# One chunk of a mixture's rows gathered behind a new wait, and normed before the next chunk is combined

## The chip, the cores and the metric

The kernel runs on one core of a Trainium2 chip. The metric is the device time of one execution in microseconds (us). The core has five engines with instruction streams of their own: TensorE (PE, with its weight loads as PEld), VectorE (DVE), ScalarE (ACT), GpSimd (POOL) and SyncE (SP, which here issues most of the DMA transfers). They wait for each other through semaphores that the kernel writes out by hand.

## The reference

Six layers are applied to an input x of 8 x 64 tokens of width 256. Each reads a layer norm of x and adds its result to x. The two that matter here are the third, a mixture of experts, and the fourth, an attention to the context with a mask:

```python
# x: (8, 64, 256) = 512 tokens; ctx_1024: (8, 1024, 256)
diff = x[:, :, None, :] - keys                      # 16 experts
logits = -jnp.sum(diff * diff, -1) + x @ rw.T + rb
topv, topi = jax.lax.top_k(logits, 4)
w = jax.nn.softmax(topv, axis=-1)
hidden = gelu(einsum('bld,efd->blef', x, w1) + b1)  # F = 1024
exp_out = einsum('blef,edf->bled', hidden, w2) + b2
fused = sum(w[..., None] * take_along_axis(exp_out, topi), axis=2)
...
logits = where(mask == 0, NEG, q @ k.T / 16)        # k = v = ctx_1024, q = layernorm(x)
out = layernorm(softmax(logits) @ v) * gamma + beta
```

## The kernel before

The 512 tokens are four chunks of 128 (TC = 4, numbered t or p). X holds x, 128 partitions by four chunks.

**The mixture.** Tokens are sorted to their experts in tiles of 128 rows. There are 31 tiles (TILES), and each has 8 units (UNITS) of a first product (`up`), a gelu on ACT (line 1298, semaphore gelu_done, one count a unit) and a second product (`down`). The first 29 tiles (COLD = 29) are copied to an SBUF tile and stored to y_slots in HBM by POOL (`store_tile`, semaphores y_stored, one for each of four buffers). The last two tiles never go to HBM: ACT takes them to SBUF (`take_last`, semaphore last_taken) and PE adds them to the chunks by a product with a spread of the gates (`add_last`). That sum lies in two banks. When the second `add_last` is done, bias_done has its counts, and DVE adds the banks to X (`add_sums`, line 2008: first chunk 0 alone, then chunks 1 to 3).

What was stored comes back by **gathers**: `gather_rows(t)` issues four indirect DMAs on POOL (one for each of a token's four experts, 128 rows of 1 KB each, line 995) that read y_slots into y_rows, and count gathered[t]. `combine(t)` on DVE waits for gathered[t] and adds the four to chunk t of X with their gates, one after the other (line 1980).

**The next attention.** For each chunk: `norm_begin(4, t)` on DVE takes the statistics (lines 1546, 1550, 1554), POOL raises the variance to the power -1/2 (`rstd_of(4, t)`, line 699), and `arrive(t)` on DVE makes the normed chunk xn (line 1558) and adds beta to X (line 2015). PE turns xn (line 2551), ACT takes it to xnT (line 1247), and PE makes the scores of chunk p from xnT and ctxT2[p] (`score2`, 16 products of 512 columns); `greatest(p)` on DVE finds their maximum (line 1986), ACT takes the exponent (line 1317), PE turns the weights (line 2738), ACT takes them to SBUF (line 1324), PE multiplies by ctxN2[p] (`mix2`, 32 products), and `normalise(p)` and `leave(p)` on DVE norm the result and begin the next layer. The order on ACT is by hand too: the exponent of chunk 2 (`weights2(2)`) stands ahead of `take_tokens(3)`, so xnT of chunk 3 waits for the maximum of chunk 2. On PE the order is: scores 0, scores 1, weights 0 turned, mix 0, weights 1 turned, scores 2, mix 1, scores 3, weights 2 turned, mix 2. The scores of chunk 0 are preceded by a few products that only keep PE running (`keep_running`).

**The context.** SP loads each chunk's part as two transfers of 2 MB: `context_T(p)` (line 600, for the scores) and `context_N(p)` (line 604, for the mix). T(0) and N(0) go behind tiles 26 and 27. T(1) goes when the last row tile has been stored. T(2) and N(1) go when gathered[2] has its count. T(3), N(2) and N(3) go when all four chunks of X are combined (x_updated, raised by DVE after `combine(3)`).

Of the kernel before, what the change touches and what calls it, by code (L numbers as in the profile page):

```python
# [32 lines left out]
E0, TOP0, F0 = 16, 4, 1024  # L33
# [7 lines left out]
UNITS = FC  # L41
OVER = E0 - 1
TILES = E0 + OVER
WB, HB, YB = 5, 4, 4
# [79 lines left out]
def part(tile, layout, name):  # L124
    a, b = layout[name]
    return tile[:, a:b]
# [29 lines left out]
def build(nc, d, out):  # L156
    ctx = ExitStack()
    with ctx:
        names = set()

        def sem(name):
            assert name not in names
            names.add(name)
            return ctx.enter_context(nc.semaphore(name))
# [300 lines left out]
        y_stored = [sem(f"y_stored{k}") for k in range(YB)]  # L465
        gathered = [sem(f"gathered{t}") for t in range(TC)]
# [8 lines left out]
        up_done, gelu_done, down_done = sem("up_done"), sem("gelu_done"), sem("down_done")  # L475
# [70 lines left out]
        def y_stores(k):  # L546

            return 16 * len(range(k, COLD, YB))

        def norm_of(k, t):  # L550

            return TC * (k - 1) + t + 1
# [23 lines left out]
        def _(sp):  # L576
# [12 lines left out]
            def expert(i):  # L589
                if i < E0:  # L590
                    of = d["w0"][i]
                else:
                    if i == E0:
                        sp.wait_ge(slots_ready, 2)
                    e = sp.value_load(owner[0:1, i - E0:i - E0 + 1], min_val=0, max_val=E0 - 1)
                    of = d["w0"][bass.ds(e, 1)].rearrange("a p n -> p (a n)")
                sp.dma_start(raw[i % WB][:], of).then_inc(raw_loaded[i % WB], 16)

            def context_T(p):
                sp.dma_start(ctxT2[p][:], d["ctxT"][2 * p:2 * p + 2].rearrange("b p c n -> p b c n"))\  # L600
                    .then_inc(ctxT2_loaded[p], 16)

            def context_N(p):
                sp.dma_start(ctxN2[p][:], d["ctxN"][2 * p:2 * p + 2].rearrange("b p k n -> p b k n"))\
                    .then_inc(ctxN2_loaded[p], 16)
# [15 lines left out]
            def masks(of):  # L621
                for m in of:
                    sp.dma_start(mask[m][:], d["mask"][m * P:(m + 1) * P]).then_inc(mask_loaded, 16)
# [7 lines left out]
            def slot_rows(k):  # L631
                a, b = X_PIECES[k:k + 2]
                sp.dma_start(x_rows[:, a - ROWS_FROM:b - ROWS_FROM, :], x_slots.rearrange("(t p) n -> p t n", p=P)[:, a:b, :]).then_inc(rows_loaded[k], 16)
# [3 lines left out]
            for i in range(TILES):  # L637
                sp.wait_ge(down_done, UNITS * (i + 1))
                if i and i + WB < TILES:
                    expert(i + WB)  # L640
                if i == PLAIN:
                    sp.wait_ge(spread_turned, share_before + LAST)
                    slot_rows(2)
                if i == TILES - WB:
                    masks(range(2, TC))
                if i == TILES - WB:
                    context_T(0)
                if i == TILES - WB + 1:
                    context_N(0)
                if i == COLD - 1:  # L650
                    sp.wait_ge(y_stored[i % YB], 16 * (i // YB + 1))
                    context_T(1)

            sp.wait_ge(gathered[2], 16 * TOP0)
# [38 lines left out]
        def _(pool):  # L693
            order = Order(pool, pool_step)

            def rstd_of(k, t):

                pool.wait_ge(var_ready, norm_of(k, t))
                nc.gpsimd.tensor_tensor(rstd[:, t:t + 1], vareps[:, t:t + 1], part(table, TABLE, "minus_half")[:, 0:1], ALU.pow)\
                    .then_inc(rstd_ready, 1)  # L700
# [291 lines left out]
            def gather_rows(t, places=range(TOP0)):  # L992
                for j in places:
                    k = TOP0 * t + j
                    nc.gpsimd.indirect_dma_start(y_rows[:, k, :], None, y_slots, bass.IndirectOffsetOnAxis(slots[:, k:k + 1], 0))\
                        .then_inc(gathered[t], 16)
# [10 lines left out]
            for k in range(YB):  # L1007
                pool.wait_ge(y_stored[k], y_stores(k))
            gather_rows(0)
            gather_rows(1)  # L1010
            pool.wait_ge(last_taken, last_before + LAST)
            gather_rows(2, range(2))
            rstd_of(4, 0)
            gather_rows(2, range(2, 3))
            rstd_of(4, 1)
            gather_rows(2, range(3, TOP0))
            gather_rows(3)
            rstd_of(4, 2)
            rstd_of(4, 3)
# [96 lines left out]
        def _(act):  # L1116
# [75 lines left out]
            def last_batch(b):  # L1192
                second_half(b - 1, 6)
                weights1(b, 0)
                second_half(b - 1, 7)
                weights1(b, 1)
                _, c, half = KEY_TURN[0]
                key_piece(key_at(b, 0), c, half)
                for d in range(1, DUOS):
                    both_halves(b, 2 * d - 2)  # L1200
                    weights1(b, 2 * d)
                    weights1(b, 2 * d + 1)
                    second_half(b, 2 * d - 1)
                    if d == 1:
                        take_front(0)
                        take_front(1)
                for half in range(2):
                    turned_half1(b, 6, half, LAST_TURN_BANKS[half], sixth_ready)
                second_half(b, 7)
# [332 lines left out]
        def _(dve):  # L1542
            order = Order(dve, dve_step)

            def norm_stats(k, t):
                nc.vector.bn_stats(stats[:, t, :], X[:, t, :]).then_inc(stats_ready, 1)

            def norm_moments(k, t):
                dve.wait_ge(stats_ready, norm_of(k, t))
                nc.vector.bn_aggr(moments[:, t, :], stats[:, t, :]).then_inc(moments_ready, 1)  # L1550

            def norm_variance(k, t):
                dve.wait_ge(moments_ready, norm_of(k, t))
                nc.vector.tensor_scalar_add(vareps[:, t:t + 1], moments[:, t, 1:2], EPS).then_inc(var_ready, 1)

            def norm_tile(k, t):
                dve.wait_ge(rstd_ready, norm_of(k, t))
                nc.vector.tensor_scalar(xn[:, t, :], X[:, t, :], moments[:, t, 0:1], rstd[:, t:t + 1],  # L1558
                                        ALU.subtract, ALU.mult).then_inc(xn_ready, 1)
# [8 lines left out]
            def norm_begin(k, t):  # L1568

                norm_stats(k, t)  # L1570
                norm_moments(k, t)
                norm_variance(k, t)
# [127 lines left out]
            def last_batch(b, par):  # L1700
# [6 lines left out]
                norm_tile(2, 2)  # L1707
                gather(b - 1, 1 - par, 0)
                _, c, half = KEY_TURN[0]
                key_piece(4 * b + len(FIRST_BANKS) + 1, c, half)  # L1710

# [265 lines left out]
            def combine(t):  # L1977
                dve.wait_ge(gathered[t], 16 * TOP0)
                for j in range(TOP0):
                    order.step(nc.vector.scalar_tensor_tensor(X[:, t, :], y_rows[:, TOP0 * t + j, :], gate_top[:, t, j:j + 1],  # L1980
                                                              X[:, t, :], ALU.mult, ALU.add))
# [24 lines left out]
            def add_sums(a, b):  # L2006
                dve.wait_ge(bias_done, (b + 1) // 2)
                order.step(nc.vector.tensor_tensor(X[:, a:b, :], X[:, a:b, :],
                                                   banks[:, 2:4, :].rearrange("p a (t n) -> p (a t) n", n=D)[:, a:b, :], ALU.add))

            def arrive(t):

                norm_tile(4, t)
                dve.wait_ge(xn_ready, norm_of(4, t))
                order.mark(nc.vector.tensor_tensor(X[:, t, :], X[:, t, :], part(rows, ROWS, "beta"), ALU.add))
# [4 lines left out]
                norm_tile(5, p)  # L2020

            combine(0)
            combine(1)
            add_sums(0, 1)
            norm_begin(4, 0)
            add_sums(1, TC)
            norm_begin(4, 1)
            arrive(0)
            arrive(1)
            greatest(0)  # L2030
            combine(2)
# [236 lines left out]
        def _(pe):  # L2268
# [157 lines left out]
            def last_batch(b, par):  # L2426
# [3 lines left out]
                weigh(b - 1, 1 - par, 0, 2)  # L2430
                turn(b - 1, 7)
                _, c, half = KEY_TURN[0]
                project_keys(key_at(b, 0), b, par, c, half)
                weigh(b - 1, 1 - par, 0, 3)
# [700 lines left out]
```

## Time and profile before

| | |
|---|---|
| median of 3 runs | 719.49 us (719.39 to 720.48) |
| the profiled execution | 718.73 us |
| its span in the trace | 716.9 us |
| PE busy | 678.7 us, 95% of the span |
| DVE, POOL, ACT busy | 544.9, 451.1, 413.8 us |
| HBM read, written | 111.77 MB, 10.81 MB |
| TensorE clock granted, mean | 0.992 |

The span is the stretch between the first and the last instruction of the trace; the 1.8 us beside it lie around it. The busy times are sums over the whole execution. The change sits in one stretch of some 60 us (480 to 540 us from the span's start), so the rows further down are from there. "T(2)" below is the transfer that `context_T(2)` issues, and so on; "gather 2.0" is the first of the four of `gather_rows(2)`.

### The profile page before, as it was taken

What the parts mean: (1) busy time and instruction counts of PE and PEld (TensorE: products, weight loads), DVE (VectorE), ACT (ScalarE), POOL (GpSimd) and SP (SyncE); (2) the same over time, 40 slices, a digit from 0 to 9 for tenths busy, and PEclk for the clock granted to TensorE, in tenths of its full rate; (3) what the DMA queues carried; (4) which work ended last, traced back from release to release, by engine and by line L of the source; (5) the groups of instructions that cost most, each with busy time, mean ns of one, the idle gap of its engine ahead of it and who ended that gap; (6) DMA issues with size and microseconds to landing.
All of it is one profiled execution on the core that took longest, in us unless ns stands there. A gap on an engine that the chain in (4) does not pass through costs nothing.

```text
span 716.9 us, 15536 instructions
## 1 busy us (share of the span) xinstructions
PE 678.7 (95%) x5712; PEld 555.4 (77%) x5712; DVE 544.9 (76%) x1212; ACT 413.8 (58%) x790; POOL 451.1 (63%) x487
## 2 busy tenths in 40 slices
PE   6899999999999978899999999999999899999998
PEld 3677777777877767799999999997457466666687
DVE  5878778787889675477777777763658899999577
ACT  3665756656755652376766766652335886665441
POOL 4848634547486734768999777835414699898130
PEclk9999999999999999999999999999999999999999
DMA  8301101001007464499999999995784620001000
GB/s 339 129 2 60 60 1 59 22 37 59 0 0 299 180 278 193 169 372 406 427 382 350 332 336 346 337 356 187 288 348 155 214 83 0 1 1 45 1 0 30
DMA packets 20365, 123.38 MB, mean 172 GB/s; under 512 B 2304, under 2 KB 6672, under 8 KB 13008
## 3 DMA queue, kind: packets, MB, share of 16 engines
q1 hardware_dynamic: 17376, 114.59, 41.6%
q0 software_dynamic: 2928, 8.00, 3.0%
q8 instruction: 35, 0.57, 0.3%
q14 instruction: 26, 0.21, 0.1%
HBM read 111.77 MB, written 10.81 MB: 171 GB/s over the span
## 4 chain that ended last, share of the span: by engine, by line
PE 78%; DVE 11%; ACT 5%; issue 3%; POOL 1%; another core or an unknown queue 1%; DMA 1%; DVEq 0%; SPq 0%; ACTq 0%; PEldq 0%; POOLq 0%
PE banks L2270 67%; PE banks L2338 8%; DVE shown L2136 2%; PE banks L2902 2%; ACT probs L1147 1%; DVE negmax_raw L1666 1%; DVE spread L1911 1%; PE banks L2579 1%; ACT banks L1437 1%; DVE banks L2143 1%; DMA table<-in_table 1%; DVE xn L1558 1%; PE banks L2738 0%; POOL q_heads_hi L711 0%
## 5 line engine op out<-in xcount | busy, mean ns | idle before, releaser
L2270 PE MATMUL banks<-xT,raw 128*128 128x128 f32 x992 | 151.4, 276 | 5.5 <-DVE xT L1921 4.9
L2270 PEld LDWEIGHTS banks<-xT,raw 128*128 128x128 f32 x992 | 134.5, 192 | 8.7 <-issue 6.8
L972 POOL TENSOR_TENSOR w_lo<-raw,w_hi 128x1024 fp32r<-128x1024 f32 x52 | 122.7, 2385 | 7.6 <-ACT w_hi L1267 7.2
L1298 ACT ACTIVATE banks<-banks,later 128x128 f32<-128x128 f32 x208 | 70.5, 340 | 56.6 <-PE banks L2270 55.4
L1930 DVE CAST mid_hi<-banks 128x128 fp32r<-128x128 f32 x208 | 60.1, 289 | 37.1 <-ACT banks L1298 34.9
L1177 ACT ACTIVATE probsT<-banks 128x512 f32<-128x512 f32 x68 | 40.1, 598 | 74.8 <-PE banks L2338 74.5
L1047 POOL TENSOR_TENSOR inject<-BCbc,drive 128x1024 f32<-128x1024 f32 x31 | 72.8, 2361 | 11.3 <-DVE shown L2136 6.3
L1147 ACT ACTIVATE probs<-banks,negmax 128x1024 f32<-128x1024 f32 x64 | 71.2, 1113 | 11.9 <-DVE negmax L1668 10.0
L1666 DVE TENSOR_REDUCE negmax_raw<-banks 128x1 f32<-128x1024 f32 x64 | 77.5, 1212 | 0.5 <-PE banks L2270 0.3
L2270 PE MATMUL banks<-w_hi,mid_hi 128*128 128x256 f32 x208 | 75.5, 363 | 0.0
L2338 PE MATMUL banks<-table,probs 128*128 128x128 f32 x512 | 69.6, 279 | 0.4 <-DVE probsT L1639 0.4
L2338 PEld LDWEIGHTS banks<-table,probs 128*128 128x128 f32 x512 | 55.1, 141 | 16.9 <-issue 14.0
L1932 DVE TENSOR_TENSOR mid_lo<-banks,mid_hi 128x128 fp32r<-128x128 f32 x208 | 60.6, 292 | 7.1
L2270 PE MATMUL banks<-w_hi,mid_lo 128*128 128x256 f32 x208 | 58.6, 282 | 0.0
L2270 PE MATMUL banks<-w_lo,mid_hi 128*128 128x256 f32 x208 | 58.5, 281 | 0.0
L1267 ACT ACTIVATE w_hi<-raw 128x1024 fp32r<-128x1024 f32 x52 | 54.6, 1050 | 0.0
L732 POOL TENSOR_TENSOR ctx_lo<-ctx_raw,ctx_hi 128x1024 fp32r<-128x1024 f32 x14 | 34.2, 2450 | 23.0 <-ACT ctx_hi L1133 22.9
L1437 ACT ACTIVATE banks<-delta,exp_a 128x512 f32<-128x512 f32 x64 | 41.6, 683 | 8.1 <-DVE shown L2153 6.0
L1639 DVE COPY probsT<-banks 128x512 f32<-128x512 f32 x60 | 41.2, 687 | 1.5 <-PE banks L2338 1.5
L1620 DVE SCALAR_TENSOR_TENSOR k_lo<-banks,bk,k_hi 128x512 fp32r<-128x512 f32 x32 | 23.8, 747 | 21.5 <-ACT k_hi L1139 21.5
L2270 PE MATMUL banks<-probsT,V 128*32 128x128 f32 x1024 | 40.0, 277 | 0.0
L2270 PEld LDWEIGHTS banks<-w_hi,mid_hi 128*128 128x128 f32 x208 | 39.9, 192 | 0.0
(362 smaller groups left out, 1709.6 us busy)
## 6 DMA issues: line engine op xcount, KB each, us to landing
raw<-in_w SPq DMA_DIRECT2D x31, 2048.0 KB, 9.3
ctx_raw<-in_ctxT SPq DMA_DIRECT2D x8, 1024.0 KB, 4.8
ctxT<-in_ctxT SPq DMA_DIRECT2D x4, 2048.0 KB, 9.0
ctxN<-in_ctxN SPq DMA_DIRECT2D x4, 2048.0 KB, 13.8
x_slots<-zero SPq DMA_DIRECT2D x1, 3968.0 KB, 12.6
y_slots<-y_tile POOLq DMA_DIRECT2D x29, 128.0 KB, 7.0
wf<-in_w SPq DMA_DIRECT2D x9, 384.0 KB, 5.9
BCbc<-bc_rows SPq DMA_DIRECT2D x6, 512.0 KB, 7.1
```

The source lines that it names most:

```text
L972: nc.gpsimd.tensor_tensor(w2_lo[i % WB][:, cols], raw[i % WB][:, EW // 2:][:, cols], w2_hi[i % 2][:, cols].bitcast(F32), ALU.subtract).the ...
L1047: nc.gpsimd.tensor_tensor(inject[g % 2][:], Bbc[:, GS * g:GS * (g + 1), :], over(drive[:, m, :], GS, 1), ALU.mult).then_inc(inject_ready, 1)
L1147: nc.scalar.activation(probs[i % 2][:], two(i % 2), ACT.Exp, bias=negmax[i % 2][:], scale=0.25, accum_out=sums[i // PAIRS][:, i % PAIRS:i ...
L1267: nc.scalar.activation(w2_hi[i % 2][:, cols], raw[i % WB][:, EW // 2:][:, cols], ACT.Copy).then_inc(w2_hi_ready, 1)
L1298: nc.scalar.activation(to, held, ACT.Gelu, bias=b1[:, bass.ds(at + u, 1)]).then_inc(gelu_done, 1)
L1437: last = nc.scalar.activation(two(HELD_BANKS[g % 2])[:, s * TOK:(s + 1) * TOK], delta[:, m, :], ACT.Copy, scale=exp_a[:, at:at + 1])
L1639: nc.vector.tensor_copy(probsT[c][:, 0:KC // 2, j, :], pb(5).rearrange("p (k n) -> p k n", n=P))\
L1666: nc.vector.tensor_reduce(negmax_raw[i % 2][:], two(i % 2), AX.X, ALU.max, negate=True).then_inc(raw_max, 1)
L1930: nc.vector.tensor_copy(mid_hi[n % HB][:], held).then_inc(mid_hi_ready, 1)
L1932: nc.vector.tensor_tensor(mid_lo[n % HB][:], held, mid_hi[n % HB][:].bitcast(F32), ALU.subtract).then_inc(mid_lo_ready, 1)
L2270: return nc.tensor.matmul(o, lhsT, rhs, start=start, stop=stop)
L2338: last = nc.tensor.transpose(pb(banks[half])[:, k * P:(k + 1) * P], probs[i % 2][:, kc * P:(kc + 1) * P], ident)
```

## The change

SP waits for the landing of chunk 0's gathers, not for the last store of a tile, before it issues T(1). POOL waits between the gathers of chunk 0 and those of chunk 1 until all but three gelus of the mixture are done. POOL's `rstd_of(4, 0)` moves from behind gather 2.1 to ahead of gather 2.0, and `rstd_of(4, 1)` from behind gather 2.2 to behind gather 2.1. DVE combines chunk 1 only after chunk 0 is normed and `arrive(0)` is done. No work is added or taken away.

```diff
@@ SP
                 if i == COLD - 1:
-                    sp.wait_ge(y_stored[i % YB], 16 * (i // YB + 1))
+                    sp.wait_ge(gathered[0], 16 * TOP0)
                     context_T(1)
@@ POOL
             gather_rows(0)
+            pool.wait_ge(gelu_done, TILES * UNITS - 3)
             gather_rows(1)
+            rstd_of(4, 0)
             pool.wait_ge(last_taken, last_before + LAST)
             gather_rows(2, range(2))
-            rstd_of(4, 0)
-            gather_rows(2, range(2, 3))
             rstd_of(4, 1)
-            gather_rows(2, range(3, TOP0))
+            gather_rows(2, range(2, TOP0))
             gather_rows(3)
@@ DVE
             combine(0)
-            combine(1)
             add_sums(0, 1)
             norm_begin(4, 0)
             add_sums(1, TC)
+            arrive(0)
+            combine(1)
             norm_begin(4, 1)
-            arrive(0)
             arrive(1)
             greatest(0)
             combine(2)
```

POOL's instructions from the last two stores on, before (-) and after (+), where the lines L995 are the gathers:

```order
 L990 DMA y_slots<-y_tile_141 128x256
 L990 DMA y_slots<-y_tile_138 128x256
-L995 DMA y_rows<-y_slots,slots 128x256 x10
-L699 TENSOR_TENSOR rstd<-vareps,table 128x1
-L995 DMA y_rows<-y_slots,slots 128x256
-L699 TENSOR_TENSOR rstd<-vareps,table 128x1
-L995 DMA y_rows<-y_slots,slots 128x256 x5
+L995 DMA y_rows<-y_slots,slots 128x256 x8
+L699 TENSOR_TENSOR rstd<-vareps,table 128x1
+L995 DMA y_rows<-y_slots,slots 128x256 x2
+L699 TENSOR_TENSOR rstd<-vareps,table 128x1
+L995 DMA y_rows<-y_slots,slots 128x256 x6
```

Ten gathers stood ahead of the first rstd and eight do now; six gathers, not five, stand behind the second.

DVE's instructions from chunk 0's statistics on; the three rows of line 1546, 1550 and 1554 that move are chunk 1's:

```order
 L1554 TENSOR_SCALAR vareps<-moments 128x1
 L2008 TENSOR_TENSOR X<-X,banks 128x768
-L1546 BN_STATS stats<-X 128x6
-L1550 BN_AGGR moments<-stats 128x2
-L1554 TENSOR_SCALAR vareps<-moments 128x1
 L1558 TENSOR_SCALAR xn<-X,moments,rstd 128x256
 L2015 TENSOR_TENSOR X<-X,rows 128x256
+L1980 SCALAR_TENSOR_TENSOR X<-y_rows,gate_top,X 128x256 x4
+L1546 BN_STATS stats<-X 128x6
+L1550 BN_AGGR moments<-stats 128x2
+L1554 TENSOR_SCALAR vareps<-moments 128x1
 L1558 TENSOR_SCALAR xn<-X,moments,rstd 128x256
```

Chunk 1's four additions and its statistics now stand between chunk 0's `arrive` and its own; the four stood ahead of `add_sums` before.

## Rows read from the trace of the kernel before

**Rows 1.** The page's first part: busy time of the engines.

```profile
PE 678.7 (95%) x5712; PEld 555.4 (77%) x5712; DVE 544.9 (76%) x1212; ACT 413.8 (58%) x790; POOL 451.1 (63%) x487
```

**Rows 2.** The chain that ended last: start us, us, what.

```profile
494.12 0.72 issue
...
528.36 3.65 PE banks L2270 x16
```

**Rows 3.** Timeline of PE and PEld: start us, us, engine, line, [idle before <-releaser].

```profile
503.24 0.38 PEld L2551 LDWEIGHTS banks<-table,xn 128*128 128x128 f32 x2 [0.43 <-DVE xn L1558]
...
508.01 0.44 PE L2551 MATMUL banks<-table,xn 128*128 128x128 f32 x2
...
523.77 3.65 PE L2270 MATMUL banks<-ctxN,probsT 128*64 128x256 f32 x32
```

**Rows 4.** Timeline of POOL.

```profile
484.42 1.05 POOL L995 DMA_INDIRECT y_rows<-y_slots,slots  x1 [3.18 <-DMA y_slots<-y_tile]
...
488.29 0.95 POOL L995 DMA_INDIRECT y_rows<-y_slots,slots  x1 [0.30 <-issue]
...
498.82 0.96 POOL L995 DMA_INDIRECT y_rows<-y_slots,slots  x1 [4.58 <-ACT y_tile L1280]
...
501.22 0.57 POOL L699 TENSOR_TENSOR rstd<-vareps,table 128x1 f32<-128x1 f32 x1 [0.18 <-DVE vareps L1554]
501.97 0.99 POOL L995 DMA_INDIRECT y_rows<-y_slots,slots  x1 [0.18 <-issue]
...
503.80 0.99 POOL L995 DMA_INDIRECT y_rows<-y_slots,slots  x1 [0.18 <-issue]
...
508.88 0.95 POOL L995 DMA_INDIRECT y_rows<-y_slots,slots  x1 [0.30 <-issue]
```

**Rows 5.** Timeline of DVE.

```profile
494.83 4.13 DVE L1980 SCALAR_TENSOR_TENSOR X<-y_rows,gate_top,X 128x256 f32<-128x256 f32 x8 [10.83 <-DMA y_rows<-y_slots,slots]
499.85 0.42 DVE L2008 TENSOR_TENSOR X<-X,banks 128x256 f32<-128x256 f32 x1 [0.88 <-PE banks L2270]
...
501.06 0.94 DVE L2008 TENSOR_TENSOR X<-X,banks 128x768 f32<-128x768 f32 x1
...
502.78 0.40 DVE L1558 TENSOR_SCALAR xn<-X,moments,rstd 128x256 f32<-128x256 f32 x1
...
515.70 2.05 DVE L1980 SCALAR_TENSOR_TENSOR X<-y_rows,gate_top,X 128x256 f32<-128x256 f32 x4 [0.80 <-DMA y_rows<-y_slots,slots]
...
518.57 0.15 DVE L1554 TENSOR_SCALAR vareps<-moments 128x1 f32<-128x1 f32 x1
...
524.34 1.22 DVE L1986 TENSOR_REDUCE stat<-banks 128x1 f32<-128x1024 f32 x1
```

**Rows 6.** Timeline of ACT.

```profile
494.43 0.37 ACT L1298 ACTIVATE mid<-banks,later 128x128 f32<-128x128 f32 x1 [2.87 <-PE banks L2270]
...
525.78 1.11 ACT L1317 ACTIVATE probs<-banks,stat 128x1024 f32<-128x1024 f32 x1 [5.61 <-DVE stat L1987]
...
527.83 0.38 ACT L1247 ACTIVATE xnT<-banks 128x256 f32<-128x256 f32 x1 [0.84 <-PE banks L2551]
```

**Rows 7.** Timeline of SP's DMA issues: T(1), then N(1).

```profile
484.21 0.37 SPq L600 DMA_DIRECT2D ctxT<-in_ctxT  x1
...
507.07 0.51 SPq L604 DMA_DIRECT2D ctxN<-in_ctxN  x1
```

**Rows 8.** DMA issues, 500 to 512 us: size, us to landing.

```profile
ctxT<-in_ctxT SPq DMA_DIRECT2D x1, 2048.0 KB, 9.0
ctxN<-in_ctxN SPq DMA_DIRECT2D x1, 2048.0 KB, 14.5
```

**Rows 9.** Stretches: busy PE, PEld, DVE, ACT, POOL; PE clock, DMA share, GB/s.

```profile
283.00:284.70 1.70, 0.00 (x0) 0.00 (x0) 0.54 (x3) 0.37 (x1) 0.00 (x0) 1.00 0.21 77
292.10:295.10 3.00, 0.00 (x0) 0.00 (x0) 2.91 (x4) 0.00 (x0) 2.84 (x2) 1.00 0.69 295
296.50:299.50 3.00, 3.00 (x12) 2.64 (x11) 0.00 (x0) 0.74 (x2) 2.08 (x4) 0.50 0.27 96
```

## The prediction

> **What bounds the kernel now.** I read the page's busy times first: PE is busy 95% of the span [rows 1], so time is lost or won only where PE waits. Then the chain of waits through the stretch that the change touches, 480 to 540 us. It stays on PE but for short steps over ACT. Two pieces matter. At 494.12 PE stands for 0.72 us, and at 528.36 the scores of chunk 3 begin [rows 2]. Then the timelines, engine by engine, for how much room each supplier of PE has.
>
> Six facts come out of them. (a) In the last tile ACT is idle for 2.87 us ahead of a gelu at 494.43 [rows 6]. The row names PE as releaser, but PE's product for it was done long before. The 0.72 us of PE just ahead are its echo. Those are the microseconds in which T(1), issued at 484.21 [rows 7], and eight gathers, issued from 484.42 on [rows 4], share the DMA engines. (b) DVE's first additions start at 494.83, when gather 0.3, issued at 488.29 to 489.24, has landed [rows 4, 5]. They end at 498.96 and then wait 0.88 us for PE's bank, so their late start costs nothing. (c) Chunk 0's xn is ready at 503.18 and its weight load at 503.24 waited for it [rows 3, 5]. (d) POOL issues gather 2.0 at 498.82, gather 2.3 at 503.80 and gather 3.3 at 508.88 [rows 4]. (e) T(2) and N(1) leave when gather 2.3 has landed, N(1) at 507.07. It lands 14.5 us later, at 521.6 [rows 7, 8], and PE wants it at 523.77 [rows 3]: 2.2 us of room. (f) Gather 3.3 was issued by 509.83, yet `combine(3)` had to wait for its landing until 515.70 [rows 4, 5]. From there DVE runs on, with only its trips to POOL between, to `greatest(2)` at 524.34 [rows 5]. ACT's exponent follows at 525.78 to 526.89, and ACT takes chunk 3's tokens at 527.83 [rows 6]: 0.9 us of room.
>
> **The change part by part.** I time it as if PE stood where it stands before, and subtract a gain at the end.
>
> *T(1) behind gathered[0].* Gathers that meet no transfer land about 1.8 us after their issue ends: gather 2.3 ends at 504.79 and the issues of T(2) and N(1), which wait for it, follow 0.4 us apart, N(1) at 507.07 [rows 4, 7]. So gathers 0.0 to 0.3 land near 491.1 and T(1) goes then, not at 484.21. With the 9.0 us of T(2) [rows 8] it lands near 500, against its first use behind 508.01 [rows 3]. The cover is 8 us. Free.
>
> *The gelu wait.* The counted gelu is the one ahead of the stall, done near 491.6. Gather 1.0 goes at 491.6, not 489.54 (four spacings of 1.25 on from 484.42), and 1.3 is issued by 496.4. It meets T(1). The worst the trace shows for that is the 5.9 us of gather 3.3, which met T(2) and N(1); at that price chunk 1's rows are there at 502.3, and with no meeting at 498.2. Needed: 502.9 (below). Free, with 0.6 us of cover at the bad end.
>
> *What the two may give.* If the stall of (a) comes of the crowded DMA engines, it shrinks: at 491 to 493 only the head of T(1) is under way. The gain is between 0 and the 0.72 us of PE. No row says which, and I take 0.4.
>
> *Chunk 0 normed first.* `arrive(0)` no longer has chunk 1's statistics ahead of it. `add_sums` ends at 502.0 [rows 5], so xn is ready at 502.4, not 503.18. PE's weight load had waited 0.43 us [rows 3]. This gives PE up to 0.4 us at 503, but everything PE wins here it loses again if it must wait later for something that does not move with it. It is not in the sum.
>
> *POOL's queue.* This is the term that counts. `rstd_of(4, 0)` waits for DVE, which waits for PE's bank; it ran at 501.22 and cannot run sooner [rows 4, 5]. Gather 2.0 was ahead of it at 498.82 and is behind it now. It goes 0.75 us after it, at 501.97, and 2.1 at 503.2. Then `rstd_of(4, 1)` waits for chunk 1: DVE ends `add_sums` at 502.0, xn 0.40 and beta about as much to 502.9, four additions of 2.05 in all to 504.9, statistics 0.95 (517.75 to 518.72) [rows 5] to 505.9. The rstd runs then, and gather 2.2 goes at 506.6, 2.3 at 507.9 and 3.3 five-quarter microseconds times four later, at 512.9. Before they were 503.80 and 508.88: **both are 4.0 us later**. Six gathers are queued behind the wait, and T(2), N(1) and the end of X behind them. (Chunk 1's own xn comes at 507.0, still ahead of 508.01.)
>
> *What is late next.* T(2) and N(1) leave 4.0 us later. T(2) lands near 519.7, just ahead of its use at 520.3. N(1) lands at 525.6, against 523.77: PE waits 1.8 us, and mix 1 ends that much later. Gather 3.3 stands to T(2) as before (3.0 goes 1.6 us ahead of it, 3.1 0.3), so it meets the same crowd and lands 4.0 us later, at 519.7. `combine(3)` and all of (f) move by 4.0, the exponent of chunk 2 ends at 530.9, ACT takes chunk 3's tokens then, not at 527.83, and the scores of chunk 3 start at 531.5, not 528.36. That is 4.0 - 0.9 = **3.1 us later**, and it contains the 1.8 of N(1): behind mix 1 PE waits the other 1.3. T(3) goes at 521.8 and by the 9.0 lands at 530.8, just in time. Behind that PE's own chain follows one for one.
>
> *Sum.* 3.1 - 0.4 = +2.7 us. Bank, rstd and gathers all start from PE's last `add_last`, so a gain of 0.4 there moves them all. The profiled execution of before took 718.73 us (span 716.9), which gives 721.4; the median of the runs is 0.76 above it, so I forecast **722.2**. Bounds of the unknowns: a gain of 0 gives 722.6, of 0.72 gives 721.9; chunk 1's rows landing later than 502.9 would add their excess.
>
> **A rule against a row.** Gather 3.3 took 5.9 us from the end of its issue to its use, with 4 MB of context issued from 3.2 us before its issue ended [rows 4, 5, 7]. This is a row and the sum goes by it. If small transfers took turns fairly with large ones they would land in about the 1.8 us of (e), at 511.6 before and 515.7 after; then (f) would not move at all. The Trainium skill, DMA: Bandwidth & Descriptors, section "Queues, rings and completion order", says that each DMA engine goes round its queues a packet at a time. By that rule gather 3.3 would not be late and the sum would be N(1)'s 1.8 us alone. The trace does not agree as to the landing, 5.9 us against 1.8.
>
> **The rivals.**
> *Only N(1) is late.* The gathers of chunk 3 could slip in ahead of T(2) by a race of tenths of a microsecond, and land by 515.7. Then +1.8 less the 0.4: 720.9. Against: the spacing of the issues is the same within 0.1 us.
> *The clock falls.* PE was idle from 292.10 to 295.10, and in 296.50 to 299.50 its clock was 0.50, half of full speed, 1.2 GHz; after 1.7 idle microseconds at 283 it stayed at 2.4 GHz [rows 9]. Three microseconds at half clock cost 1.5: 723.8. Here the gaps are 1.8 and 1.3 with work between, nearer the one that kept the clock. The Trainium skill, TensorE: Matmul & The Clock Gate, section "Part 1: The HAM clock gate", has idleness as what closes the gate; which of the two gaps ours resembles only rows can tell.
> *Not slower.* The stall at 494 vanishes (-0.72), the earlier xn gives its 0.4, and the 4 us of POOL are hidden. For that N(1) would have to land in 12.7 us instead of 14.5 and gather 3.3 in 2.7 instead of 5.9, that is, the DMA engines would have to be emptier than before. It decides if POOL's delay stays under 0.9 us, the room of (f). Time: 718.4, or a little below if the gelus gain more.
> *No change at all in the order that matters:* excluded, POOL's stream shows the gathers behind the rstd.
>
> **How the numbers follow.** A run of this kernel can tell about 0.2%, 1.4 us, from no change: 718.1 to 720.9. Both waits, 721.9 to 722.7: 0.56. Only N(1): 0.14, on the border, half in "same". Clock: 0.10. Not slower: 0.20, of which 0.08 beyond 0.2%. So faster 0.08, same 0.19, slower 0.73. The range leaves out most of the last case and the far end of the clock's: 720.2 to 724.2.
>
> **What would show it.** Right: gathers 2.0 and 3.3 at about 501.6 and 512.5; DVE's `combine(3)` starting near 519.3; PE idle some 1.8 us ahead of mix 1 for the context and 1.3 ahead of the scores of chunk 3 for ACT; PE's 0.72 us at 494 smaller; the clock at 1.00. Wrong: `combine(3)` at 516, N(1) landing by 523, or the chain of waits still without a gap between 504 and 532.

## The result, and the profile after

The changed kernel takes **720.89 us**, the median of 20 runs (719.37 to 723.11), beside 718.70 us for the kernel before, the median of 20 runs on the same chip (717.36 to 721.13): ratio 1.003, 95% interval 1.002 to 1.004. It is slower by 2.2 us; the forecast was +2.7 in the profiled execution and 722.2 us for the median.

718.70 is 0.8 below the median shown ahead of the prediction, so differences say more here than absolute times. The profiled execution of the changed kernel is the slowest of its 20, 723.11 us with a span of 721.3. Part of that has nothing to do with the change: T(0) is issued at 470.01 us, against 467.58 before, though the program is the same up to there. Positions are therefore compared from an event, not from the start: from T(0)'s issue, or, where the prediction counts that way, from DVE's first addition of PE's bank (499.85 before [rows 5], 501.29 after).

PE of the changed kernel: start us, us, engine, line, [idle before <-releaser].

```profile
498.55 1.03 PE L2270 MATMUL banks<-raw,mid 128*128 128x256 f32 x4
500.05 1.99 PE L2270 MATMUL banks<-y_tile,spreadT 128*128 128x256 f32 x8 [0.47 <-ACT y_tile L1280]
...
505.87 3.65 PE L2270 MATMUL banks<-ctxT,xnT 128*64 128x512 f32 x16 [0.56 <-ACT xnT L1247]
...
510.46 3.65 PE L2270 MATMUL banks<-ctxT,xnT 128*64 128x512 f32 x16
...
517.40 3.67 PE L2270 MATMUL banks<-ctxN,probsT 128*64 128x256 f32 x32 [2.26 <-ACT probsT L1324]
...
523.20 3.65 PE L2270 MATMUL banks<-ctxT,xnT 128*64 128x512 f32 x16 [0.42 <-ACT xnT L1247]
527.00 3.67 PE L2270 MATMUL banks<-ctxN,probsT 128*64 128x256 f32 x32
```

The four groups of ctxT are scores 0 (505.87), 1 (510.46), 2 (523.20) and, below in the chain, 3; the two of ctxN are mix 0 (517.40) and mix 1 (527.00). The 0.72 us of PE [rows 2] are gone. There is a new wait of 2.26 us ahead of mix 0, where the kernel before waits 0.83 for the same probsT. Mix 1 shows no wait worth a row, although its context landed at the last moment (below).

POOL, then DVE, then ACT of the changed kernel:

```profile
494.26 0.94 POOL L995 DMA_INDIRECT y_rows<-y_slots,slots  x1 [1.94 <-ACT mid L1298]
495.51 1.07 POOL L995 DMA_INDIRECT y_rows<-y_slots,slots  x1 [0.30 <-issue]
...
502.66 0.57 POOL L699 TENSOR_TENSOR rstd<-vareps,table 128x1 f32<-128x1 f32 x1 [3.59 <-DVE vareps L1554]
503.42 0.99 POOL L995 DMA_INDIRECT y_rows<-y_slots,slots  x1 [0.18 <-issue]
504.71 0.96 POOL L995 DMA_INDIRECT y_rows<-y_slots,slots  x1 [0.31 <-issue]
507.26 0.57 POOL L699 TENSOR_TENSOR rstd<-vareps,table 128x1 f32<-128x1 f32 x1 [1.59 <-DVE vareps L1554]
508.02 0.99 POOL L995 DMA_INDIRECT y_rows<-y_slots,slots  x1 [0.18 <-issue]
...
514.35 0.95 POOL L995 DMA_INDIRECT y_rows<-y_slots,slots  x1 [0.30 <-issue]
```

```profile
501.29 0.42 DVE L2008 TENSOR_TENSOR X<-X,banks 128x256 f32<-128x256 f32 x1 [5.02 <-PE banks L2270]
...
521.00 2.05 DVE L1980 SCALAR_TENSOR_TENSOR X<-y_rows,gate_top,X 128x256 f32<-128x256 f32 x4 [3.90 <-DMA y_rows<-y_slots,slots]
```

```profile
494.50 0.37 ACT L1298 ACTIVATE mid<-banks,later 128x128 f32<-128x128 f32 x1 [0.51 <-PE banks L2270]
...
496.26 0.37 ACT L1298 ACTIVATE mid<-banks,later 128x128 f32<-128x128 f32 x1 [0.51 <-PE banks L2270]
...
515.22 0.60 ACT L1324 ACTIVATE probsT<-banks 128x512 f32<-128x512 f32 x1 [2.39 <-PE banks L2738]
516.65 0.60 ACT L1324 ACTIVATE probsT<-banks 128x512 f32<-128x512 f32 x1 [0.84 <-PE banks L2738]
```

Gather 3.3 is issued at 514.35, 13.06 us behind the bank's first addition; before it was 508.88, 9.03 behind [rows 4, 5]. `combine(3)` starts 19.71 behind it, not 15.85. The page's DMA view for the stretch 505 to 520 us of the changed kernel gives N(1), issued at 512.56, 14.4 us to its landing, that is 526.96, and mix 1's weight load waited for it:

```profile
ctxN<-in_ctxN SPq DMA_DIRECT2D x1, 2048.0 KB, 14.4
```

```profile
527.00 3.22 PEld L2270 LDWEIGHTS banks<-ctxN,probsT 128*64 128x64 f32 x32 [1.02 <-DMA ctxN<-in_ctxN]
```

The chain that ended last (start us, us, what) tells the same in one piece. Where before it kept to PE but for short steps over ACT, it now leaves PE at the bank's addition and comes back only at scores 3:

```profile
500.05 1.15 PE banks L2270 x4
501.29 0.43 DVE X L2008
...
507.26 0.57 POOL rstd L699
507.83 0.18 issue
508.02 0.99 POOL y_rows L995
...
514.35 6.63 DMA y_rows<-y_slots,slots
521.00 0.50 DVE X L1980
...
532.30 0.28 ACT xnT L1247
532.58 0.14 issue
532.72 3.65 PE banks L2270 x16
```

The account, in us from T(0)'s issue. The last column is gather 3.3's own issue. "Last additions" is PE's second `add_last`.

| kernel (T(0) issued at) | last additions | scores 0 | mix 0 | scores 2 | mix 1 | scores 3 | gather 3.3 |
|---|---|---|---|---|---|---|---|
| before (467.58) | 31.03 | 36.84 | 46.94 | 52.74 | 56.19 | 60.78 | 41.30 |
| after (470.01) | 30.04 | 35.86 | 47.39 | 53.19 | 56.99 | 62.71 | 44.34 |

One microsecond (0.99) is won by the last additions. Behind them 2.92 are lost in three places: 1.43 at mix 0 (scores 1 are still 0.98 ahead), 0.35 at mix 1 and 1.13 at scores 3. The net, 62.71 - 60.78 = 1.93, stands beside the 2.19 of the medians.

### The profile page after: what moved, and what is told of

The parts are those of the page before. It is cut to its first block, busy times and chain, and to the rows that moved or that the text cites. A ratio compares the mean times of both kernels' runs of the same rounds, so it can differ in the third digit from the quotient of the medians.

```text
span 721.3 us, 15536 instructions
## 1 busy us (share of the span) xinstructions
PE 680.7 (94%) x5712; PEld 556.6 (77%) x5712; DVE 540.9 (75%) x1212; ACT 413.7 (57%) x790; POOL 450.5 (62%) x487
## 4 chain that ended last, share of the span: by engine, by line
PE 76%; DVE 12%; ACT 4%; issue 3%; DMA 2%; POOL 1%; another core or an unknown queue 1%; DVEq 0%; SPq 0%; ACTq 0%; PEldq 0%
PE banks L2270 64%; PE banks L2338 8%; DVE shown L2136 2%; PE banks L2902 2%; DMA ctx_raw<-in_ctxT 1%; ACT probs L1147 1%; DVE negmax_raw L1666 1%; DMA y_rows<-y_slots,slots 1%; PE banks L2579 1%; DVE xn L1558 1%; ACT banks L1437 1%; POOL y_rows L995 1%; DVE banks L2143 1%; POOL rstd L699 1%
## 5 line engine op out<-in xcount | busy, mean ns | idle before, releaser
L2270 PEld LDWEIGHTS banks<-w_lo,mid_hi 128*128 128x128 f32 x208 | 40.2, 193 | 0.0
```

The costliest lines, as they stand in the source:

```text
L2270: return nc.tensor.matmul(o, lhsT, rhs, start=start, stop=stop)
```

## The experiments

Ratios are to the kernel before, run beside it on the same chip, with the 95% interval. "Changed" in a heading means that the edit is made to the changed kernel, otherwise to the kernel before. Their medians of the kernel before were 718.56 (22 runs), 719.24 (23) and 719.80 (29) us.

**order_only: changed, without the two waits.** T(1) goes behind `y_stored` as before, and POOL does not wait for a gelu.

```diff
-                    sp.wait_ge(gathered[0], 16 * TOP0)
+                    sp.wait_ge(y_stored[i % YB], 16 * (i // YB + 1))
-            pool.wait_ge(gelu_done, TILES * UNITS - 3)
```

> The change without its two waits on transfers: T(1) goes behind the last store and gathers 0 and 1 run through, as before; the order of DVE and POOL is the changed one. Theory A (the loss is POOL's queue: gathers 2.2 to 3.3 stand behind the rstd of chunk 1; the gain is that T(1) no longer crowds the last tile): gather 3.3 about 4.0 us later than in the kernel before, counted from the bank that DVE waits for, combine(3) as much, and no gain at the last tile, so +2.9 us, ratio 1.004. Rival B (the loss comes from chunk 1's gathers and T(1) meeting between 495 and 503): no loss, ratio 1.000 within 0.1%.

Measured 721.8 us (7 runs), ratio 1.0038 [1.0023, 1.0053]. The whole loss is there without the waits: it sits in the order of POOL and DVE. The last additions come 0.47 earlier than before, not 0.99 (none was expected), and ACT's stall at the last gelus is there (2.04, 1.10 and 1.10 us). In its profiled execution the clock rival shows itself: PE stands 2.06 us ahead of mix 0 and then does the 32 products in 5.36 us, not 3.67. Beside them the columns of the stretch (busy PE, PEld, DVE, ACT, POOL; PE clock, DMA share, GB/s), for this kernel and then for the profiled execution of the changed one over the same products, which it did at full clock:

```profile
517.47 5.36 PE L2269 MATMUL banks<-ctxN,probsT 128*64 128x256 f32 x32 [2.06 <-ACT probsT L1323]
```

```profile
517.50:520.80 3.30, 3.30 (x20) 2.41 (x22) 0.00 (x0) 0.92 (x2) 0.00 (x0) 0.61 1.02 416
```

```profile
517.50:520.80 3.30, 3.30 (x32) 2.51 (x31) 0.00 (x0) 0.85 (x2) 0.00 (x0) 1.00 1.03 418
```

**filled: changed, with the gathers spread around the two rstds.** DVE's order and both waits stay. Three gathers still stand behind chunk 1's rstd, but POOL does not stand idle ahead of it: no other could have gone first without making the rstd late.

```diff
             gather_rows(0)
             pool.wait_ge(gelu_done, TILES * UNITS - 3)
             gather_rows(1)
-            rstd_of(4, 0)
             pool.wait_ge(last_taken, last_before + LAST)
             gather_rows(2, range(2))
-            rstd_of(4, 1)
+            rstd_of(4, 0)
             gather_rows(2, range(2, TOP0))
-            gather_rows(3)
+            gather_rows(3, range(1))
+            rstd_of(4, 1)
+            gather_rows(3, range(1, TOP0))
```

> The changed kernel with one thing altered: POOL's two rstds are put where they fall due, rstd of chunk 0 behind gather 2.1 and that of chunk 1 behind gather 3.0, so that the gathers of chunks 2 and 3 run in the time in which POOL waited. Theory A: gather 2.3 and 3.3 come as early, from the bank, as in the kernel before (3.3 within 0.5 us), PE's idle time ahead of the scores of chunk 3 is gone, and the gain at the last tile is left: 0.7 to 1.0 us faster than before, ratio 0.999. Rival B: +2.2 us as in the changed kernel. Rival C (the rstd of chunk 1, about 1 us later than due, holds up the scores of chunk 1): +0.5.

Measured 717.77 us (11 runs), ratio 0.9988 [0.9975, 1.0001]. Gather 3.3 is issued 40.56 us behind T(0), 3.8 earlier than in the changed kernel, and all of PE's positions in the table lie 0.97 or 0.98 before those of the kernel before: last additions 30.05, scores 0 35.86, mix 0 45.96, scores 2 51.76, mix 1 55.22, scores 3 59.80. Mix 0 and scores 3 of filled:

```profile
514.56 3.67 PE L2271 MATMUL banks<-ctxN,probsT 128*64 128x256 f32 x32 [0.83 <-ACT probsT L1325]
...
528.40 3.65 PE L2271 MATMUL banks<-ctxT,xnT 128*64 128x512 f32 x16
```

So with the gathers early the 2.92 us are not lost at all, and the 0.99 stay won to the end. The wait for the gelu, T(1) late and chunk 0 first cost nothing.

**dose: changed, with all gathers of chunk 2 behind chunk 1's rstd.** Two more gathers are held.

```diff
-            gather_rows(2, range(2))
             rstd_of(4, 1)
-            gather_rows(2, range(2, TOP0))
+            gather_rows(2)
```

> The changed kernel with a larger dose: rstd of chunk 1 stands ahead of all gathers of chunk 2, so gathers 2.0 and 2.1 wait too. Theory A: gathers 2.3 and 3.3 another 2.5 us later, and the end with them one for one: +4.5 to +4.9 us against before, ratio 1.0065. Rival B: as the changed kernel, 1.003.

Measured 724.95 us (5 runs), ratio 1.0087 [1.0069, 1.0105]: +6.4 us. Gather 3.3 is issued at 46.92 behind T(0), 2.6 later than changed, and scores 3 come at 66.18, 3.5 later. More than the dose asks, and the trace shows the rest: T(2) is now late too, and scores 2 run at half clock behind the gap.

```profile
520.74 5.35 PE L2269 MATMUL banks<-ctxT,xnT 128*64 128x512 f32 x16 [2.35 <-DMA ctxT<-in_ctxT]
...
532.64 3.65 PE L2269 MATMUL banks<-ctxT,xnT 128*64 128x512 f32 x16 [2.26 <-ACT xnT L1246]
```

So the forecast of 4.5 to 4.9 us was too small. Scores 3, behind a gap of 2.26 us, ran at full clock.

**sp_only: T(1) behind gathered[0], nothing else.** The test of what the prediction called the cause of the stall.

```diff
-                    sp.wait_ge(y_stored[i % YB], 16 * (i // YB + 1))
+                    sp.wait_ge(gathered[0], 16 * TOP0)
```

> The kernel before with only T(1) moved behind gathered[0]. Theory A: ACT's idle time of 2.9 us in the last tile falls to the 0.5 us of its neighbours and PE's 0.7 us with it, nothing else moves: 0.5 to 1.0 us faster, ratio 0.999. Rival D (ACT's idle time has another cause and its absence in the changed kernel was chance): 1.000. Against both: if gather 1 meets T(1) and lands after DVE needs chunk 1, up to +1.

Measured 722.44 us (10 runs), ratio 1.0054 [1.0034, 1.0075]. A miss. T(1) leaves at 492.46, in the middle of ACT's stall, and the stall is not smaller but larger. ACT and then PE of sp_only:

```profile
495.84 0.37 ACT L1298 ACTIVATE mid<-banks,later 128x128 f32<-128x128 f32 x1 [3.83 <-PE banks L2270]
```

```profile
496.26 0.70 PE L2270 MATMUL banks<-raw,mid 128*128 128x256 f32 x2 [1.68 <-ACT mid L1298]
...
507.96 5.35 PE L2270 MATMUL banks<-ctxT,xnT 128*64 128x512 f32 x16 [0.57 <-ACT xnT L1247]
```

It loses once more behind: the rows of chunk 1 now meet T(1), DVE takes them in the old order ahead of chunk 0's sums, and scores 0 come late, behind a gap of 1.91 us ahead of chunk 0's xn, and at half clock. The move of T(1) alone is harmful; it needs chunk 0 normed first.

**gelu_only: POOL's wait for the gelu, nothing else.**

```diff
             gather_rows(0)
+            pool.wait_ge(gelu_done, TILES * UNITS - 3)
             gather_rows(1)
```

> The kernel before with only the gelu wait between the gathers of chunk 0 and chunk 1; T(1) goes early, as before, and meets the gathers of chunk 0. Theory E (ACT's idle time in the last tile comes with the gathers of chunk 1 being issued then, not with T(1)): ACT's 2.9 us and PE's 0.7 us are gone although T(1) is early. Rival F (it comes with T(1)): they stay. Either way chunk 1's rows land near 498.5, its four additions stand ahead of the bank's, and chunk 0's xn comes about 0.5 to 1.5 us late: 1.000 to 1.002 by theory E, 0.001 more by rival F.

Measured 720.01 us (12 runs), ratio 1.0013 [1.0002, 1.0024]. T(1) leaves early, at 485.72, and the stall is gone all the same. ACT there, with no idle time over 0.51 us from 491 to 495 (the 2.63 us ahead of the gelu at 490.15 stand in every kernel, before and after, at that gelu):

```profile
491.90 0.37 ACT L1299 ACTIVATE mid<-banks,later 128x128 f32<-128x128 f32 x1 [0.24 <-PE banks L2271]
492.78 0.37 ACT L1299 ACTIVATE mid<-banks,later 128x128 f32<-128x128 f32 x1 [0.51 <-PE banks L2271]
```

The last additions come 0.62 earlier, and the kernel is no faster, because chunk 1's rows, later now, hold up chunk 0 in the old order: its xn comes 1.06 us late for PE at 504.79.

**calm: both waits in the old order.** The diff is that of sp_only and gelu_only together.

> Both waits of the change, with the order of DVE and POOL as before. Chunk 1's rows meet T(1) and land 2.0 us behind the bank that DVE waits for, as in the trace of the changed kernel, and here chunk 0 cannot be normed before they are added. Theory G (the reorder on DVE is what lets the two waits be had): chunk 0's xn 4 us later, PE idle for about 3 us behind its running products, ratio 1.004 to 1.007, worse than the changed kernel. Rival: PE's running products cover most of it, 1.001.

Measured 723.74 us (6 runs), ratio 1.0058 [1.0038, 1.0078]. No stall, last additions 1.0 earlier, and then PE waits for chunk 0's xn long enough to come back at half clock:

```profile
506.79 0.69 PE L2552 MATMUL banks<-table,xn 128*128 128x128 f32 x2 [3.71 <-DVE xn L1559]
508.04 6.08 PE L2271 MATMUL banks<-ctxT,xnT 128*64 128x512 f32 x16 [0.56 <-ACT xnT L1248]
```

filled has the same two waits with chunk 0 first (and chunk 1's rstd two gathers later on POOL), and stands at 0.9988, some 5 us below the 1.0058 of calm. So chunk 0 first, which the sum counted as nothing, is worth about that much once both waits are in; no run moves it alone.

**filled_nowait: filled, without the wait for the gelu.**

```diff
-            pool.wait_ge(gelu_done, TILES * UNITS - 3)
```

> The kernel with the filled queue of POOL (rstds placed where due), T(1) behind gathered[0], DVE's changed order, but without the gelu wait. Theory E: ACT's idle time of 2 to 4 us in the last tile is back and PE loses 0.7 to 1.7 us there: 1.000 to 1.001 against before, 0.001 to 0.002 worse than the filled one. Rival F (it comes with T(1), which is late here): as the filled one, 0.999.

Measured 719.72 us (12 runs), ratio 1.0012 [0.9998, 1.0027]. ACT stands again at the last gelus, 2.10 and 2.48 us, and the last additions come at 31.34, 1.29 later than in filled.

```profile
492.18 0.37 ACT L1298 ACTIVATE mid<-banks,later 128x128 f32<-128x128 f32 x1 [2.10 <-issue]
495.03 0.37 ACT L1298 ACTIVATE mid<-banks,later 128x128 f32<-128x128 f32 x1 [2.48 <-remote]
```

**filled_m6: filled, with the wait three gelus earlier.** POOL hardly waits (gather 1.0 starts 0.30 us behind 0.3).

```diff
-            pool.wait_ge(gelu_done, TILES * UNITS - 3)
+            pool.wait_ge(gelu_done, TILES * UNITS - 6)
```

> The filled kernel with the gelu wait at all but six gelus instead of all but three, so that chunk 1's gathers start about 1 us or more earlier and two or three of them are issued ahead of the three gelus at which ACT stood idle. Theory E2 (ACT stands when gathers have been issued just ahead of that point): part of ACT's idle time is back and PE loses 0.2 to 0.7 us: 0.999 to 1.000. Rival (only a full queue of eight gathers does it): as the filled one, 0.9988.

Measured 720.37 us (12 runs), ratio 1.0012 [0.9997, 1.0028], 2.2 us above filled, which ran beside it (filled_again below). The stalls are back (1.49, 2.52 and 1.09 us), last additions at 31.41. So it is not enough that a wait is there: it must make POOL pause. As POOL's eight gathers went out without a pause here, as in filled_nowait, the run does not tell whether fewer than eight would do it, which it was meant to. The traces give 1.36 us of the 2.2; the rest has no row.

**late_ctx: changed, with T(2) and N(1) behind gathered[3].** It separates the two things that the prediction hung on POOL: the issue of gather 3.3, and what it meets.

```diff
-            sp.wait_ge(gathered[2], 16 * TOP0)
+            sp.wait_ge(gathered[3], 16 * TOP0)
```

> The changed kernel with T(2) and N(1) held until gather 3.3 has landed. Theory H (gather 3.3 lands late because the context's 4 MB are issued ahead of the last three gathers): it lands about 1.8 us after its issue ends instead of 5.7, and combine(3) starts 4 us earlier; T(2) and N(1) leave about 4 us later and PE waits for them, 1.5 to 3 us: 1.004 to 1.006. Rival (queues take turns, the landing is late for another reason): combine(3) starts as in the changed kernel and the waits come on top, 1.008.

Measured 723.86 us (6 runs), ratio 1.0064 [1.0047, 1.0082]. POOL, DVE and PE of late_ctx:

```profile
512.77 0.95 POOL L995 DMA_INDIRECT y_rows<-y_slots,slots  x1 [0.30 <-issue]
```

```profile
515.56 2.05 DVE L1980 SCALAR_TENSOR_TENSOR X<-y_rows,gate_top,X 128x256 f32<-128x256 f32 x4
```

```profile
515.71 5.36 PE L2270 MATMUL banks<-ctxN,probsT 128*64 128x256 f32 x32 [2.15 <-ACT probsT L1324]
...
524.43 3.65 PE L2270 MATMUL banks<-ctxT,xnT 128*64 128x512 f32 x16 [1.66 <-DMA ctxT<-in_ctxT]
529.40 3.67 PE L2270 MATMUL banks<-ctxN,probsT 128*64 128x256 f32 x32 [1.31 <-DMA ctxN<-in_ctxN]
```

Alone on the DMA engines, gather 3.3 is used 1.8 us after its issue ended (513.72 to 515.56), where in the changed kernel it took 5.7 (515.30 to 521.00). The price is that the context comes late in three places (the third, ahead of scores 3, is 0.47 us), and mix 0 runs at half clock.

This kernel is the changed one up to the last gelus, with both waits, and yet ACT stands at them. Its gathers of chunk 0 went out about 1 us later, so POOL paused for 0.98 us, not 1.94. The last additions come at 30.61, not 30.04. POOL, then ACT:

```profile
492.11 0.95 POOL L995 DMA_INDIRECT y_rows<-y_slots,slots  x1 [0.98 <-issue]
```

```profile
492.90 0.37 ACT L1298 ACTIVATE mid<-banks,later 128x128 f32<-128x128 f32 x1 [1.06 <-PE banks L2270]
494.41 0.37 ACT L1298 ACTIVATE mid<-banks,later 128x128 f32<-128x128 f32 x1 [1.14 <-PE banks L2270]
```

**filled_again and changed_again: the same two kernels once more, side by side.**

> The filled kernel once more, beside the changed kernel on one chip. Theory A: 0.9988 again, within 0.001, so that both together exclude 1. Rival: its first result was chance, 1.000.

> The changed kernel itself, beside the filled one. 1.003 as measured before; by theory A it is 2.9 to 3.1 us above the filled one.

Measured 718.14 us (12 runs), ratio 0.9973 [0.9957, 0.9989], and 720.57 us (12 runs), ratio 1.0015 [0.9999, 1.0031]. filled beats both kernels, the changed one by 2.4 us where 2.9 to 3.1 were expected. The changed kernel itself came out only 0.8 us above the kernel before, with an interval that just includes 1, where the first 20 runs gave 2.2 us; the two intervals overlap. The second profiled execution of the changed kernel differs from the first at one place: mix 0 ran at half clock.

```profile
514.53 5.36 PE L2270 MATMUL banks<-ctxN,probsT 128*64 128x256 f32 x32 [2.21 <-ACT probsT L1324]
...
530.30 3.65 PE L2270 MATMUL banks<-ctxT,xnT 128*64 128x512 f32 x16 [0.34 <-ACT xnT L1247]
```

Its scores 3 come at 63.06 from T(0), against 62.71: the 1.7 us of half clock fill most of what PE would have waited for ACT there.

## Why the prediction was right, and where it was not

*POOL's queue: right, and to a tenth.* Forecast from the bank's addition: gather 2.3 at 8.05 us and 3.3 at 13.05; measured 8.03 and 13.06. The six gathers stand behind chunk 1's rstd, 4.03 us late. filled issues three of them ahead of it, so that gather 3.3 goes 0.74 earlier than before, and the loss is gone; dose adds two and it grows. This is the cause, shown both ways.

*Gather 3.3 meets the same crowd: right.* `combine(3)` was forecast 4.0 later and is 3.86 later; late_ctx shows that it is the 4 MB of context that make 5.7 us out of 1.8. The rule against the row, turns of a packet at a time in the Trainium skill, DMA: Bandwidth & Descriptors, section "Queues, rings and completion order", had gather 3.3 land in time; the row decided rightly here.

*What is late next: right in place and size.* From the bank's addition, N(1) was forecast to land 4.0 later and lands 3.95 later; mix 1 starts 1.79 later, forecast 1.8; scores 3 start 2.92 later, forecast 3.1. But the wait that mix 1 was to show is not there. ACT took probsT of chunk 0 late, PE stood 1.43 us longer ahead of mix 0, and only 0.35 was left for N(1) to cost. As chunk 3's end was set by gather 3.3 anyway, this unforecast stall cost nothing by itself. Why ACT stood there is open: it did in four traces in which POOL issued its six late gathers just then (after, order_only, late_ctx, changed_again), not in before or filled, but not in dose either, where POOL issued eight at that time. So the gathers alone do not explain it, and no run was made for it. T(3), the other thing that scores 3 wait for, was issued at 523.19 and took 8.7 us, to 531.9; xnT was ready 0.7 later, at 532.58, and decided.

*The gain: the mis-sized term.* "I take 0.4", between 0 and 0.72; it measured 0.99 at the last additions. The 0.72 of [rows 2] is only what the profile marks as idle. From the start of PE's last product ahead of the stall to the start of the first `add_last` it is 1.85 us before (493.53 to 495.38) and 0.87 after (495.96 to 496.83), and those 0.98 are the gain. It hangs on one trace of the kernel before: in the four other traces in which POOL does not pause, the last additions come between 30.56 and 32.00.

The reason given for the stall was wrong as well. It was put on DMA engines crowded by T(1) and eight gathers. sp_only took T(1) out of the crowd and the stall grew, gelu_only left T(1) in it and the stall went, and filled_nowait and filled_m6, in which POOL does not pause, have it again. What goes with the stall is whether POOL pauses between the gathers of chunk 0 and those of chunk 1: with none (0.30 us, as between any two gathers) it is in all five traces, with 0.98 us it is there in part (late_ctx), and with 1.80 to 2.00 us in none of seven. It is not the issue of a gather by itself: the changed kernel's gathers 1.0 and 1.1 (494.26 and 495.51) go out while its last three gelus run on time. How the one acts on the other is open. That the number came near was luck of the bounds; of the change's two waits only the gelu's did good at this place.

*Nothing for T(1), the gelu wait and chunk 0 first: right together, not apart.* In filled all three cost nothing. Without chunk 0 first, the waits cost 0.8 us (gelu_only), 3.9 (sp_only) and 4.5 (both, calm): the 0.6 us of cover that the prediction gave chunk 1's rows holds only because `arrive(0)` no longer waits for them. The 8 us of T(1) held everywhere: scores 1 wait for no context in any run.

*The clock: a rival that was half right.* It did not happen in the profiled execution of the changed kernel, whose clock was 1.00 from 480 to 540 us, but it did in changed_again, order_only, dose and late_ctx, behind gaps of 2.06 to 2.35 us, and in sp_only behind one of 1.91, nearer to the 1.8 that the prediction took for safe. The prediction's price was 1.5 (its own sum for this rival is 723.7, not 723.8); it costs 1.7 us at its place and less at the end, as the next wait takes it up.

*Sum.* 2.92 - 0.99 = 1.93 in the traces and 2.19 in the medians, against 3.1 - 0.4 = 2.7. The gain too small by 0.6 and the loss too large by 0.2 make the difference.

## What to carry to other kernels

A queue engine that waits for a scalar of another engine holds every DMA queued behind that wait: count those DMAs, and put as many ahead of the wait as are ready, as filled does. A stall that lies beside a crowd of transfers is not thereby caused by them; move one suspect at a time. And edits that cost nothing together may each need the other: the order of DVE that the prediction priced at zero was what made the two waits affordable.

## What the runs showed of the hardware

ACT stands at gelus whose inputs PE has long written, for 1 to 4 us, in all five traces in which POOL issues eight indirect DMAs 0.30 us apart: 2.87 us before, 3.83 in sp_only, 2.04 in order_only, 2.10 and 2.48 in filled_nowait, 1.49 and 2.52 in filled_m6. With a pause of 1.80 to 2.00 us behind the fourth, none is over 0.51 at these gelus in seven traces, though the fifth and sixth DMA are issued while they run. With a pause of 0.98 (late_ctx) they are 1.06 and 1.14. In before and in sp_only the held gelu starts 0.2 us after the last gather's issue ended (494.24 and 494.43; 495.64 and 495.84), but in filled_nowait not, so what the two share stays open.

Gaps of PE of 1.91 us (sp_only), four between 2.06 and 2.35 us, and one of 3.71 (calm) were followed by products at half clock (5.36 us for what takes 3.67, 5.35 for 3.65). Two gaps of 2.26 us were not: that of the profiled changed kernel, on the same products, and that ahead of scores 3 in dose. The gap's length alone does not decide it.
